# A fused attention and adapter kernel on one core: one group of scores is issued after the next two groups of transposes instead of before them

## The chip, the cores and the metric

The kernel runs on one core of a Trainium2 chip. The metric is the device time of one execution in microseconds; lower is better. Three runs of the kernel before took 963.36, 960.85 and 961.24 us, median 961.24 us.

## What is computed

The reference applies four layers with a residual each to `x` (32 batches of 256 rows by 256 columns). Cut to what matters:

```python
x = x + attention(x, fside, lens)   # 16 heads of 16; q from fside, keys and values from x,
                                    # one own key and value per row, softmax, @ Wo
x = x + layernorm(x + relu(x @ W1[lang] + b1) @ W2[lang] + b2) * gamma[lang] + beta[lang]
x = x + x @ weight[subj].T + bias[subj]
# pooling: scores from a small tanh layer, masked by kind, softmax over 256 keys
a = tanh(x @ W1 + b1) @ v
p = softmax(where(mask[kind], a[None, :], -1e30))
x = x + (p @ x) / mask[kind].sum(-1)
```

## The kernel before, in words

The work is a software pipeline over batches. `steps` calls `step(t, parity)` for t = -2 to 34; t = 6 to 27 run as a loop of two steps a turn, the others are written out. In a steady step six batches are at work at once (`at_work`): A projects queries and keys of batch t+2, B computes row maxima and values for t+1, C the scores, exponentials and the first half of the weighted sums of t, E finishes the attention of t-1, F runs the adapter and the subject's linear layer of t-2, and G the pooling of t-3. From t = 30 on A is off, from t = 31 on B, from t = 32 on C; G is on for t = 3 to 34.

Each engine has its own order, written out by hand in its `step`. Semaphores tie them together. The names that matter here:

- **TensorE (PE).** `scores(pair)`, pair 0 to 7, issues eight matmuls on 64 or 63 rows of the array: four transposed scores of batch t into `ST` (line 515) and four plain scores of batch t+1 into `SN` (line 519), two banks each. It waits for `exp_done` and `maxed`, that is until ScalarE and VectorE have emptied those banks. `weighted(k, ...)` (line 494) is 32 matmuls on column tiles 32 wide that sum the exponentials `pt` with the values `vaug`; `weighted(0)` needs the exponentials of pairs 0 to 3 only. `turn` (line 425) is four 128x128 transposes of a 256x256 tile. The transposes of `pe3`, the pooled probabilities (the third part of the buffer `soft`), go to bank `pT`; those of `att`, the attention rows (buffer `nv`), go to `aT`; those of `yn`, the normalised rows, go to `x2T`. Projections go through `three` (line 417): `values("v", ...)` is 12 matmuls `M<-Wv,xs`, `values("vs", ...)` 12 matmuls `M<-Wv,ss`.
- **ScalarE (ACT).** `unit(s)`, s = 0 to 15, is one exponential `pt<-ST` (line 890); units 2p and 2p+1 belong to pair p. Between them stand copies out of PSUM: `keys_out` (`kf`), the high part of the weights `lwp`, the two exponentials of the pooling (line 1011, each with a second instruction that reads the accumulated sum and whose end raises the semaphore `pe3`), `values_out` (`vaug`), the copy of the transposed probabilities `p3T` (shown as `soft<-M`), of `aT`, and the two `yn` (line 1029).
- **VectorE (DVE).** `unit(s)` is one row maximum `mx<-SN` (line 1132). `fold_join(2)` exists at t = 0 and 1 only.

The order of TensorE around the change, before:

```python
                scores(4)
                ...
                    own_scores()
                    values("v", xs[odd], W["v"])
                scores(5)
                ...
                    pe.wait_ge(sem("pe3"), done(t - 3, 2))
                    turn(bank["pT"], pe3).then_inc(sem("pT_pe"), 1)
                ...
                    turn(bank["aT"], att).then_inc(sem("aT_pe"), 1)
                ...
                    weighted(0, t, par)
                scores(6)
```

Of the kernel before, what the change touches and what calls it, by code (L numbers as in the profile page):

```python
# [74 lines left out]
def done(b, per=1, nth=None):  # L75

    nth = per if nth is None else nth
    if isinstance(b, int):
        return 0 if b < 0 else B * per if b >= B else b * per + nth
    return b * per + nth  # L80
# [7 lines left out]
def before(b, unit):  # L88

    if isinstance(b, int):  # L90
        return max(0, min(b, B) * UNITS + unit) if b < B else B * UNITS
    return b * UNITS + unit


def block4(nc: bass.Bass, x, xsT, lens, ids, wq, wk, wv, wo, wad, lw, lwT, lb, fixed_d, early_d, kidx_d,
           pmask_d, out):
    ctx = ExitStack()
    with ctx:
# [8 lines left out]
        def sem(name):  # L107
            if name not in sems:
                sems[name] = ctx.enter_context(nc.semaphore(name))
            return sems[name]  # L110
# [146 lines left out]
        def folding(t):  # L257

            return isinstance(t, int) and 0 <= t < 2
# [151 lines left out]
        def _(pe):  # L411
# [9 lines left out]
            def turn(dst, src):  # L421

                for c in range(NC2):
                    for i in range(2):
                        last = nc.tensor.transpose(dst[:, c * S + i * P:c * S + i * P + P],  # L425
                                                   src[:, i, c * P:c * P + P], ident[:])
                return last
# [35 lines left out]
            def step(t, par):  # L463
# [3 lines left out]
                def free(name):  # L467

                    k = NAMES.index(name)
                    mine, u = PIECES[k][3], t  # L470
                    while True:
                        k -= 1
                        if k < 0:
                            k, u = len(PIECES) - 1, u - 1
                        if isinstance(u, int) and u < -2:
                            return
                        _, n, o, on_bank = PIECES[k]
                        if on_bank == mine and folding(u) and n in FOLD:
                            pe.wait_ge(cat, 4 * u + FOLD.index(n) + 1)
                            return  # L480
                        if on_bank == mine and (not isinstance(u, int) or 0 <= u + o < B):
                            for s, per, nth in READER[n]:
                                pe.wait_ge(sem(s), done(u + o, per, nth))
                            return
# [14 lines left out]
                def scores(pair):  # L499

                    if on["C"] and pair % PH == 0:
                        pe.wait_ge(sem(f"mput{pair // PH}"), done(t, 64))
                    if on["B"] and pair % PH == 0:
                        pe.wait_ge(sem(f"stack{pair // PH}"), done(t + 1, SK))
                    if on["C"]:
                        pe.wait_ge(sem("exp_done"), before(t, 2 * pair))
                    opening = isinstance(t, int) and t == -1
                    rows_to = ST if opening and pair % 2 else SN
                    if on["B"]:
                        pe.wait_ge(sem("maxed"), max(0, 2 * pair - 2) if opening else before(t + 1, 2 * pair))  # L510
                    for e in range(2):
                        lo_, hi_ = 64 * e, 64 * (1 - e)
                        for half in range(2):
                            if on["C"]:
                                keys = nc.tensor.matmul(ST[e][:, half * S:half * S + S],  # L515
                                                        kst[par][lo_:lo_ + MROW + 1, pair, half * P:half * P + P],
                                                        qst[par][lo_:lo_ + MROW + 1, pair, :], start=True, stop=True)
                            if on["B"]:
                                rows_ = nc.tensor.matmul(rows_to[e][:, half * S:half * S + S],  # L519
                                                         qst[odd][hi_:hi_ + MROW, pair, half * P:half * P + P],  # L520
                                                         kst[odd][hi_:hi_ + MROW, pair, :], start=True, stop=True)
                        if on["C"]:
                            keys.then_inc(sem("st_ready"), 1)
                        if on["B"]:
                            rows_.then_inc(sem("sn_ready"), 1)
# [8 lines left out]
                def values(name, left, w):  # L534

                    for i in range(2):
                        last = three(bank[name][:, i * D:i * D + D], lambda r, c: left[r][:, c, i * P:i * P + P],
                                     lambda r, c: w[r][:, c, :])
                    last.then_inc(sem(f"{name}_pe"), 1)
# [138 lines left out]
                if on["B"]:  # L678
                    own_scores()
                    free("v")  # L680
                    values("v", xs[odd], W["v"])
                scores(5)
                if folding(t):
                    fold_next("pT")
                if on["G"]:
# [3 lines left out]
                if on["E"]:  # L689
                    free("aT")  # L690
                    pe.wait_ge(sem("att"), done(t - 1))
                    turn(bank["aT"], att).then_inc(sem("aT_pe"), 1)
                if on["C"]:
                    weighted(0, t, par)
                scores(6)
# [32 lines left out]


            steps(pe, step)  # L730


# [133 lines left out]
        def _(act):  # L866
            def copy(dst, src, bias=0.0):
                return nc.scalar.activation(dst, src, ACT.Identity, bias=bias)  # L868
# [5 lines left out]
            def halves(name):  # L874
                return bank[name][:].rearrange("p (c q) -> p c q", c=2)

            def step(t, par):
# [3 lines left out]
                def unit(s):  # L881

                    if not on["C"]:
                        return
                    g, j = s // 4, s % 4
                    act.wait_ge(sem("st_ready"), before(t, s + 1))
                    if s % 8 == 0:

                        act.wait_ge(sem("pv_done"), done(t - 1, 2, s // 8 + 1))
                    nc.scalar.activation(pt[:, g, :, j, :],  # L890
                                         ST[s % 2][:].rearrange("p (h q) -> p h q", h=2), ACT.Exp,
                                         scale=SCALE).then_inc(sem("exp_done"), 1)
# [119 lines left out]
                                             accum_out=sum3[:, i:i + 1]).then_inc(sem("pe3"), 1)  # L1012
                if on["B"]:
                    values_out()
                unit(10)
                unit(11)
                if on["G"]:
                    act.wait_ge(sem("pT_pe"), done(t - 3))
                    act.wait_ge(sem("pool_pe"), done(t - 4))
                    copy(p3T[:], halves("pT")).then_inc(sem("p3T"), 1)  # L1020
                if on["E"]:
                    act.wait_ge(sem("aT_pe"), done(t - 1))
                    act.wait_ge(sem("wo_pe"), done(t - 2))
                    copy(aT[0][:], halves("aT")).then_inc(sem("aThi"), 1)
# [27 lines left out]


            steps(act, step)


        @block.vector
        def _(dve):
# [47 lines left out]
            def step(t, par):  # L1106
# [12 lines left out]
                def maxima_turn(half, b, i):  # L1119

                    dve.wait_ge(sem(f"mneg{half}"), done(b))
                    dve.wait_ge(sem(f"mput{half}"), done(b - 1, 64))
                    nc.vector.transpose(mT[half][:], mneg[i][:].bitcast(F32)).then_inc(sem(f"mT{half}"), 1)

                def unit(s):

                    if not on["B"]:
                        return
                    dve.wait_ge(sem("sn_ready"), before(t + 1, s + 1))
                    if s < 2:  # L1130
                        dve.wait_ge(sem("earg"), done(t - 1))
                    nc.vector.tensor_reduce(out=mx[odd][:, :, 8 * (s // 8) + PH * (1 - s % 2) + s // 2 % PH],  # L1132
                                            in_=(ST if isinstance(t, int) and t == -1 and s // 2 % 2 else SN)[s % 2][:].rearrange("p (h k) -> p h k", h=2),
                                            op=ALU.max, axis=AX.X).then_inc(sem("maxed"), 1)
# [29 lines left out]
                def fold_join(j):  # L1164

                    if not folding(t):
                        return
                    name, j = FOLD[j], j + 4 * t
                    dve.wait_ge(fold, j + 1)
                    nc.vector.tensor_tensor(lw3[:, j], bank[name][:, 0:2 * A1].rearrange("p (c n) -> p c n", c=NC2),  # L1170
                                            w3s, ALU.add).then_inc(cat, 1)
# [108 lines left out]
                    nc.vector.bn_aggr(mv[:, 1, :], st[:, 1, :]).then_inc(sem("var"), 1)  # L1280
                if on["B"]:
                    maxima_turn(0, t + 1, odd)
                unit(10)
                unit(11)
                fold_join(2)
                if on["G"]:

                    dve.wait_ge(sem("pe3"), done(t - 3, 2))
# [107 lines left out]
```

## Time and profile before

| what | value |
|---|---|
| median of three runs | 961.24 us (960.85 to 963.36) |
| the profiled execution's own time | 958.85 us |
| its span, first to last instruction | 956.9 us |
| TensorE matmul busy | 915.0 us, 96% |
| VectorE, ScalarE, GpSimd busy | 73%, 67%, 64% |
| granted TensorE clock, mean | 0.979 |

The span is the time between the first and the last instruction of the profiled execution; its own time has 1.95 us more around it, and lies 2.4 us under the median of the runs. Busy time of TensorE is modelled from pipelined matmuls, so 96% says that something is nearly always in the array, and not that it runs at its peak. A timeline row gives the start of a group, how long it lasted, the engine, the line, the operation, the tiles it writes and reads, its shape and how many instructions were merged; an arrow in square brackets tells how long the engine was idle before it and who ended that.

### The profile page before, as it was taken

The numbers are of one execution on the slowest core, as the hardware profiler recorded it, in microseconds if no ns is written. First come the engines' busy times: TensorE is split into PE (matmuls) and PEld (weight loads), VectorE is DVE, ScalarE is ACT, GpSimd is POOL, SyncE is SP. The second block draws the span as 40 slices with busy tenths as digits, with TensorE's granted clock in tenths as the row PEclk, the third lists the DMA queues.
The fourth block names the chain that finished last, engine by engine and source line by source line (L and its number), as shares of the span: only waits on it lengthen the run. The fifth ranks groups of instructions, "written<-read, shape, count | busy, mean of one in ns | idle before, by whom it ended". The sixth has DMA issues, their size and how long they took to land. (4 is left out here: it accounts for less than half of the span.)

```text
span 956.9 us, 27946 instructions
## 1 busy us (share of the span) xinstructions
PE 915.0 (96%) x8564; PEld 764.2 (80%) x8564; DVE 695.3 (73%) x1608; ACT 641.1 (67%) x1377; POOL 608.0 (64%) x771
## 2 busy tenths in 40 slices
PE   8899999999999999999999999999999999999855
PEld 7787788888888888888888888888888888877544
DVE  7765777877777778777777777777777777776442
ACT  2355677777677777776777777767777776677541
POOL 5333777767666777666676766666777676655551
PEclk9999999999999999999999999999999999999876
DMA  5544335344433444444334444443353444432311
GB/s 199 173 138 142 114 110 158 128 147 156 132 126 114 143 142 139 146 145 134 117 122 148 138 133 156 139 130 122 119 156 126 145 156 135 122 108 74 96 43 34
DMA packets 113193, 124.55 MB, mean 130 GB/s; under 512 B 23525, under 2 KB 95094, under 8 KB 113142
## 3 DMA queue, kind: packets, MB, share of 16 engines
q1 hardware_dynamic: 111846, 122.44, 40.5%
q10 hardware_dynamic: 1296, 1.46, 0.5%
q8 instruction: 27, 0.44, 0.2%
q14 instruction: 24, 0.20, 0.1%
HBM read 64.05 MB, written 8.96 MB: 76 GB/s over the span
## 5 line engine op out<-in xcount | busy, mean ns | idle before, releaser
L1132 DVE TENSOR_REDUCE mx<-SN 128x2 f32<-128x512 f32 x504 | 324.1, 685 | 72.4 <-PE SN L519 72.2
L890 ACT ACTIVATE pt<-ST 128x512 f32<-128x512 f32 x512 | 278.1, 599 | 81.1 <-PE ST L515 79.3
L515 PE MATMUL ST<-qst,kst 64*128 64x256 f32 x1024 | 187.9, 305 | 12.2 <-DVE mx L1132 4.5
L515 PEld LDWEIGHTS ST<-qst,kst 64*128 64x128 f32 x1024 | 136.1, 186 | 68.0 <-issue 26.4
L519 PE MATMUL SN<-kst,qst 63*128 63x256 f32 x1008 | 184.2, 305 | 0.1
L519 PEld LDWEIGHTS SN<-kst,qst 63*128 63x128 f32 x1008 | 132.8, 186 | 0.8 <-issue 0.4
L494 PE MATMUL PV<-pt,vaug 128*32 128x256 f32 x2048 | 125.1, 385 | 0.0
L748 POOL TENSOR_TENSOR ss<-xsin,ss 128x512 fp32r<-128x512 f32 x32 | 41.4, 1292 | 121.9 <-ACT ss L868 113.9
L494 PEld LDWEIGHTS PV<-pt,vaug 128*32 128x32 f32 x2048 | 60.4, 110 | 43.7 <-issue 6.6
L417 PE MATMUL M<-lwp,x2T 128*128 128x320 f32 x384 | 70.8, 321 | 1.0 <-DVE ob L1316 1.0
L748 POOL TENSOR_TENSOR x2T<-x2f,x2T 128x512 fp32r<-128x512 f32 x32 | 41.2, 1287 | 44.2 <-ACT x2T L868 44.2
L708 PE MATMUL M<-x,soft 128*128 128x256 f32 x256 | 65.6, 402 | 0.8 <-ACT soft L868 0.8
L748 POOL TENSOR_TENSOR xs<-xsin,xs 128x512 fp32r<-128x512 f32 x31 | 40.0, 1289 | 39.3 <-ACT xs L868 39.3
L791 POOL TENSOR_TENSOR nv<-nv,rec 128x512 f32<-128x512 f32 x32 | 34.0, 1062 | 43.2 <-DVE rec L1152 43.2
L417 PEld LDWEIGHTS M<-lwp,x2T 128*128 128x128 f32 x384 | 58.3, 193 | 1.8 <-DVE ob L1316 1.7
L417 PE MATMUL PV<-Wo,aT 128*128 128x256 f32 x384 | 56.6, 297 | 1.1 <-ACT pvt L868 1.1
L417 PE MATMUL PV<-ss,Wq 128*128 128x256 f32 x384 | 54.1, 291 | 1.9 <-POOL ss L748 1.9
L417 PE MATMUL M<-ss,Wk 128*128 128x256 f32 x384 | 55.3, 295 | 0.0
L868 ACT ACTIVATE qf<-PV,bqc 128x256 f32<-128x256 f32 x64 | 26.9, 471 | 42.4 <-PE PV L417 42.4
L708 PEld LDWEIGHTS M<-x,soft 128*128 128x128 f32 x256 | 49.5, 204 | 7.2 <-issue 1.1
L1161 DVE TENSOR_TENSOR x<-M,lbr 128x320 f32<-128x320 f32 x64 | 31.1, 486 | 32.2 <-PE M L417 32.2
L417 PE MATMUL M<-Wv,ss 128*128 128x256 f32 x384 | 53.8, 289 | 0.0
(140 smaller groups left out, 2088.1 us busy)
## 6 DMA issues: line engine op xcount, KB each, us to landing
qst<-qp SPq DMA_DIRECT2D x186, 128.0 KB
kst<-kp SPq DMA_DIRECT2D x186, 128.0 KB
xsin<-in_xsT SPq DMA_DIRECT2D x31, 512.0 KB, 3.4
adw<-in_wad SPq DMA_DIRECT2D x32, 322.5 KB, 3.9
pm<-in_pmask SPq DMA_DIRECT2D x32, 257.0 KB, 2.7
xr<-in_x SPq DMA_DIRECT2D x32, 256.0 KB, 4.2
lwf<-in_lwT SPq DMA_DIRECT2D x32, 256.0 KB, 3.1
out<-ob SPq DMA_DIRECT2D x32, 256.0 KB, 2.1
```

Of the source, the lines that this page charges most:

```text
L417: last = nc.tensor.matmul(dst, left(a, c), right(b, c), start=n == 0, stop=n == 5)
L494: last = nc.tensor.matmul(PV[32 * j:32 * j + 32, (g % 2) * S:(g % 2) * S + S], vaug[i][:, kb, 4 * g + j, :], pt[:, g, kb, j, :], start=kb ...
L515: keys = nc.tensor.matmul(ST[e][:, half * S:half * S + S], kst[par][lo_:lo_ + MROW + 1, pair, half * P:half * P + P], qst[par][lo_:lo_ + M ...
L519: rows_ = nc.tensor.matmul(rows_to[e][:, half * S:half * S + S], qst[odd][hi_:hi_ + MROW, pair, half * P:half * P + P], kst[odd][hi_:hi_ + ...
L708: last = nc.tensor.matmul(bank["pool"][:, i * D:i * D + D], p3T[:, c, i * P:i * P + P], x3[:, c, 0:D], start=c == 0, stop=c == 1)
L748: return nc.gpsimd.tensor_tensor(dst, src, high.bitcast(F32), ALU.subtract)
L791: nc.gpsimd.tensor_tensor(att[:].rearrange("p c (h d) -> p c h d", d=DH), nv[:].rearrange("p c (h d) -> p c h d", d=DH), rec[:].unsqueeze( ...
L868: return nc.scalar.activation(dst, src, ACT.Identity, bias=bias)
L890: nc.scalar.activation(pt[:, g, :, j, :], ST[s % 2][:].rearrange("p (h q) -> p h q", h=2), ACT.Exp, scale=SCALE).then_inc(sem("exp_done"), 1)
L1132: nc.vector.tensor_reduce(out=mx[odd][:, :, 8 * (s // 8) + PH * (1 - s % 2) + s // 2 % PH], in_=(ST if isinstance(t, int) and t == -1 and ...
L1161: nc.vector.tensor_tensor(x3[:, i, :], bank[f"lin{i}"][:, 0:NX], lbr[:], ALU.add).then_inc(sem("x3"), 1)
```

## The change

On TensorE `scores(5)` is issued behind the transposes of `pe3` and of `att`, directly ahead of `weighted(0)`. On ScalarE the copy `p3T` of the transposed probabilities stands ahead of units 10 and 11, the exponentials of that group of scores. On VectorE `fold_join(2)` stands ahead of its units 10 and 11. No instruction is added or removed, and every wait keeps its value.

```diff
@@ TensorE
                     values("v", xs[odd], W["v"])
-                scores(5)
                 if folding(t):
                     fold_next("pT")
                 if on["G"]:
@@
                     pe.wait_ge(sem("att"), done(t - 1))
                     turn(bank["aT"], att).then_inc(sem("aT_pe"), 1)
+                scores(5)
                 if on["C"]:
                     weighted(0, t, par)
                 scores(6)
@@ ScalarE
                 if on["B"]:
                     values_out()
-                unit(10)
-                unit(11)
                 if on["G"]:
                     act.wait_ge(sem("pT_pe"), done(t - 3))
                     act.wait_ge(sem("pool_pe"), done(t - 4))
                     copy(p3T[:], halves("pT")).then_inc(sem("p3T"), 1)
+                unit(10)
+                unit(11)
                 if on["E"]:
@@ VectorE
                     maxima_turn(0, t + 1, odd)
+                fold_join(2)
                 unit(10)
                 unit(11)
-                fold_join(2)
```

TensorE's queue in a steady step, before, from the values to the weighted sums; a row has the line, the operation, what it writes and reads, its shape and the semaphores it waits for. Of the eight matmuls of the scores the first two are shown:

```order
L417 MATMUL M<-Wv,xs 128x256 [waits y]
L417 MATMUL M<-Wv,xs 128x256 x11
L515 MATMUL ST<-qst,kst 128x256 [waits maxed,exp_done]
L519 MATMUL SN<-kst,qst 128x256
...
L425 MATMUL M<-fixed,soft 128x128 [waits pe3,kf]
L425 MATMUL M<-fixed,soft 128x128 x3
L425 MATMUL M<-fixed,nv 128x128 [waits att,nself]
L425 MATMUL M<-fixed,nv 128x128 x3
L494 MATMUL PV<-pt,vaug 32x256 [waits qf,v,exp_done]
L494 MATMUL PV<-pt,vaug 32x256 x15
```

The same place in the changed kernel:

```order
L417 MATMUL M<-Wv,xs 128x256 [waits y]
L417 MATMUL M<-Wv,xs 128x256 x11
L425 MATMUL M<-fixed,soft 128x128 [waits pe3,kf]
L425 MATMUL M<-fixed,soft 128x128 x3
L425 MATMUL M<-fixed,nv 128x128 [waits att,nself]
L425 MATMUL M<-fixed,nv 128x128 x3
L515 MATMUL ST<-qst,kst 128x256 [waits maxed,exp_done]
L519 MATMUL SN<-kst,qst 128x256
...
L494 MATMUL PV<-pt,vaug 32x256 [waits qf,v,exp_done]
L494 MATMUL PV<-pt,vaug 32x256 x15
```

The eight matmuls of `scores(5)` moved past the eight transposes; the first transpose, which waits for `pe3`, now stands directly behind the values.

ScalarE's queue at the same place of a steady step, before, from the second exponential of pair 4 on:

```order
L890 ACTIVATE pt<-ST 128x2x256 [waits st_ready]
L1011 ACTIVATE soft,sum<-soft,nm 128x256 [waits r3,pT_pe,nm3]
L1011 ACTIVATE soft,sum<-soft,nm 128x256
L868 ACTIVATE vaug<-M 128x32x16 [waits pv_done,v_pe]
L890 ACTIVATE pt<-ST 128x2x256 [waits st_ready] x2
L868 ACTIVATE soft<-M 128x512 [waits pool_pe,pT_pe]
L868 ACTIVATE aT<-M 128x512 [waits wo_pe,aT_pe]
L1029 ACTIVATE yn<-y,shift,rstd 128x256 [waits x2T_pe,shift]
```

And in the changed kernel:

```order
L890 ACTIVATE pt<-ST 128x2x256 [waits st_ready]
L1011 ACTIVATE soft,sum<-soft,nm 128x256 [waits r3,pT_pe,nm3]
L1011 ACTIVATE soft,sum<-soft,nm 128x256
L868 ACTIVATE vaug<-M 128x32x16 [waits pv_done,v_pe]
L868 ACTIVATE soft<-M 128x512 [waits pool_pe,pT_pe]
L890 ACTIVATE pt<-ST 128x2x256 [waits st_ready] x2
L868 ACTIVATE aT<-M 128x512 [waits wo_pe,aT_pe]
L1029 ACTIVATE yn<-y,shift,rstd 128x256 [waits x2T_pe,shift]
```

The copy of the transposed probabilities and the two exponentials of pair 5 have changed places; all that stands ahead of them, the pooling's two exponentials among it, is where it was.

## Rows read from the trace of the kernel before

**Rows 1.** The page: the span, and the busy time of TensorE.

```profile
span 956.9 us, 27946 instructions
PE 915.0 (96%) x8564; PEld 764.2 (80%) x8564; DVE 695.3 (73%) x1608; ACT 641.1 (67%) x1377; POOL 608.0 (64%) x771
```

**Rows 2.** Windows: stretch and its length, busy time by engine, clock, DMA share, GB/s.

```profile
480.00:508.00 28.00, 27.92 (x274) 23.50 (x272) 21.64 (x51) 20.29 (x45) 19.49 (x25) 1.00 0.46 147
860.00:866.00 6.00, 4.85 (x44) 4.07 (x43) 5.96 (x16) 3.99 (x8) 2.57 (x4) 1.00 0.49 161
```

**Rows 3.** Timeline of TensorE in one steady step: start us, us.

```profile
481.67 1.67 PE L417 MATMUL M<-Wv,xs 128*128 128x256 f32 x12
483.27 0.38 PE L515 MATMUL ST<-qst,kst 64*128 64x256 f32 x1
...
483.94 0.66 PE L425 MATMUL M<-fixed,soft 128*128 128x128 f32 x4
...
484.96 1.93 PE L494 MATMUL PV<-pt,vaug 128*32 128x256 f32 x32
486.82 0.38 PE L515 MATMUL ST<-qst,kst 64*128 64x256 f32 x1
...
487.49 0.65 PE L425 MATMUL M<-fixed,yn 128*128 128x128 f32 x4
...
491.89 1.68 PE L417 MATMUL M<-Wv,ss 128*128 128x256 f32 x12
493.41 1.05 PE L417 MATMUL M<-lwp,x2T 128*128 128x320 f32 x6
```

**Rows 4.** Timeline of ScalarE over the same step.

```profile
480.19 0.84 ACT L868 ACTIVATE kf<-M,bkc 128x256 f32<-128x256 f32 x2 [1.12 <-PE M L417]
...
481.54 1.08 ACT L890 ACTIVATE pt<-ST 128x512 f32<-128x512 f32 x2
...
483.39 0.21 ACT L1011 ACTIVATION_READ_ACCUMULATOR soft<-soft,nm 128x1 f32 x1
...
485.39 0.65 ACT L868 ACTIVATE aT<-M 128x512 fp32r<-128x512 f32 x1
485.87 1.14 ACT L1029 ACTIVATE yn<-y,shift,rstd 128x256 f32<-128x256 f32 x2
487.36 1.08 ACT L890 ACTIVATE pt<-ST 128x512 f32<-128x512 f32 x2 [0.34 <-PE ST L515]
488.33 0.60 ACT L868 ACTIVATE pvt<-PV 128x512 f32<-128x512 f32 x1
```

**Rows 5.** Timeline of ScalarE: the sum's last read at t = 3, 30 and 32.

```profile
126.00 0.21 ACT L1011 ACTIVATION_READ_ACCUMULATOR soft<-soft,nm 128x1 f32 x1
866.57 0.19 ACT L1011 ACTIVATION_READ_ACCUMULATOR soft<-soft,nm 128x1 f32 x1
911.75 0.19 ACT L1011 ACTIVATION_READ_ACCUMULATOR soft<-soft,nm 128x1 f32 x1
```

**Rows 6.** Timeline of TensorE: `scores(5)` at t = 3 and 30; t = 31; the transpose at t = 32.

```profile
125.87 0.38 PE L515 MATMUL ST<-qst,kst 64*128 64x256 f32 x1
866.67 0.38 PE L515 MATMUL ST<-qst,kst 64*128 64x256 f32 x1
889.71 0.80 PE L515 MATMUL ST<-qst,kst 64*128 64x256 f32 x4 [1.88 <-ACT pt L890]
890.78 1.09 PE L425 MATMUL M<-fixed,soft 128*128 128x128 f32 x4 [0.27 <-ACT soft L1011]
892.65 0.66 PE L494 MATMUL PV<-pt,vaug 128*32 128x256 f32 x4
912.08 0.77 PE L425 MATMUL M<-fixed,soft 128*128 128x128 f32 x4 [3.75 <-ACT soft L1011]
```

**Rows 7.** Timeline of VectorE in the same step: maxima of pair 5, low part of `aT`.

```profile
483.84 1.29 DVE L1132 TENSOR_REDUCE mx<-SN 128x2 f32<-128x512 f32 x2 [0.24 <-PE SN L519]
...
486.07 0.69 DVE L1137 TENSOR_TENSOR aT<-M,aT 128x512 fp32r<-128x512 f32 x1 [0.67 <-ACT aT L868]
```

## The prediction

> **What bounds the kernel now.** I read the page first, then the busy time by windows, then the timelines of TensorE and ScalarE around the change. The page shows TensorE busy for 915.0 of 956.9 us, and no other engine over 73% [rows 1]. The windows show that the steady part is tighter still: 27.92 of 28 us are busy, at a granted clock of 1.00, the 2.4 GHz level [rows 2]. In the timeline of one steady step the groups follow each other without an idle bracket [rows 3]: values at 481.67, `scores(5)` at 483.27, the transposes of `pe3` at 483.94, the weighted sums at 484.96, `scores(6)` at 486.82, the transposes of `yn` at 487.49. So a steady step costs what TensorE's queue costs. A wait put into that queue costs its whole length, and a wait of another engine costs nothing until TensorE stands behind it. The question is when the things that the moved groups wait for are ready.
>
> **What the first transpose waits for.** It needs `pe3`, the pooling's two exponentials, complete with their sum. ScalarE is woken for this stretch by TensorE itself, at the end of the key projection: `kf` at 480.19 after 1.12 us of idling, then without a pause `lwp`, the two exponentials of pair 4 at 481.54, the pooling's two, and the last read of the sum, which starts at 483.39 and ends at 483.60 [rows 4]. `scores(5)` starts at 483.27, so `pe3` is complete 0.33 us after that start. Today the 0.67 us of `scores(5)` hide it: the transposes start at 483.94, 0.34 us after `pe3`. At t = 3 it is the same: the read ends at 126.21, `scores(5)` starts at 125.87, 0.34 us later than which `pe3` is complete [rows 5, 6]. This distance can't drift, since the chain starts on TensorE's own key projection and has no other wait in it. At t = 30 the chain lacks `kf`, and the read ends at 866.76 against 866.67, 0.09 us [rows 5, 6].
>
> **The change, part by part.** Time zero is the present start of `scores(5)`.
>
> (1) *The lost cover.* The transposes now come where `scores(5)` was, and `pe3` is complete only at 0.33 to 0.34. From that end to the first transpose there is a further delay: at t = 32, where TensorE stands waiting for the same semaphore, the read ends at 911.94 and the transpose starts at 912.08, 0.14 us [rows 5, 6]. I take 0.14; the least would be nothing, the most would be twice that, since no row shows a longer one. The transposes start at 0.33 + 0.14 = 0.47 us.
>
> (2) *The rest of the moved block.* The two groups of transposes took 483.94 to 484.96 = 1.02 us, and `scores(5)` 483.27 to 483.94 = 0.67 us [rows 3]. They only change places: `scores(5)` starts at 0.47 + 1.02 = 1.49, the weighted sums at 1.49 + 0.67 = 2.16. Now they start at 484.96 - 483.27 = 1.69. **TensorE loses 0.47 us a step here.** Of the waits of `scores(5)` itself none is late: the exponentials of pair 4 are through by 482.62 [rows 4], 0.65 us before the place it had already.
>
> (3) *One change of the array's tiling less.* Scores use the array by 64 rows, the weighted sums by 32 columns, the rest as a whole. The order values, scores, transposes, weighted sums changes the form three times, the new one twice. Twelve matmuls take 1.60 us in front of scores (481.67 to 483.27) and 1.52 us in front of other whole-array matmuls (491.89 to 493.41) [rows 3], so a change costs about 0.1 us. Where TensorE doesn't wait, this is a gain. In steps 3 to 29 it isn't one: the change left out is the one ahead of the transposes, and it would fall into the time in which TensorE stands waiting for `pe3` anyway. I count it nought there, and 0.1 us for each of t = 0, 1 and 2, which have no pooling. The Trainium skill, TensorEngine Tiling (Array Packing), section Key Properties, says that a change of tiling mode drains TensorE. By that rule the change is worth 0.1 us a step; the trace agrees with the rule in the pair of 1.60 and 1.52 us, and it is the first rival below.
>
> (4) *What is late next: `yn`.* On ScalarE the copy of `p3T` now comes ahead of the exponentials of pair 5. It is not late: the four transposes are complete 0.66 us after 0.47 [rows 3], a copy like it takes the engine 0.48 us (485.39 to 485.87) [rows 4], so it is through at 1.6, and the exponentials can't start before 1.49 + 0.54 = 2.03. But behind those exponentials stand `aT` and the two `yn`, and they lose time. An exponential starts 487.36 - 486.82 = 0.54 us after its scores; two of them take 488.33 - 487.36 = 0.97 us until the next instruction, `aT` 0.48, both `yn` 1.14 to the end [rows 3, 4]. So `yn` is complete at 1.49 + 0.54 + 0.97 + 0.48 + 1.14 = 4.62, and with the 0.14 us of (1) its transposes can start at 4.76. TensorE is there at 2.16 + 1.86 (weighted sums) + 0.67 (`scores(6)`) = 4.69 [rows 3]. That is a second wait of 0.07 us; between nothing and 0.15 us, since all its terms are rounded. Now `yn` ends at 487.01, 0.48 us ahead of 487.49. The copy of `aT` itself, ready at 3.6, has its reader, the output projection, only after the pooling's matmuls; VectorE's low part of it takes 0.69 us [rows 7] and is in time. The maxima of pair 5 started 0.57 us behind their scores and took 1.29 us [rows 3, 7]; from 1.49 on they end at 3.35, and `scores(6)`, which overwrites their bank, comes at 2.16 + 1.86 = 4.02. What stands behind on ScalarE is again woken by `scores(6)`.
>
> (5) *Other queues.* SP and GpSimd have the same rows. VectorE's moved piece exists at t = 0 and 1 only, and its bank is read earlier than before: nothing.
>
> (6) *The sum.* Steps 3 to 29 (27 of them): 0.47 + 0.07 = 0.54, together 14.6 us. Step 30: `pe3` at 0.09 + 0.14 = 0.23 instead of 0.47, so 0.23 + 0.07 = 0.3 us. Step 31: the four matmuls of `scores(5)` ran from 889.71 while TensorE waited for ScalarE anyway, and took 0.80 us [rows 6]; now they stand behind the same wait, ahead of the weighted sums of 892.65, for 0.4 to 0.8 us: 0.6. Steps 32 to 34 have no scores. Steps 0 to 2: -0.3. Sum: **15.2 us more**. On the profiled execution that is 958.85 + 15.2 = 974.1 us; it was 2.4 us under the median of the runs, and from the median 961.24 it is **976.4 us**, which I give.
>
> **Rivals.**
>
> *The wait does not come about, and the drain is saved.* If `pe3` were in time (because what looks like a chain that ends at 0.33 is released earlier than the end of the read), 31 steps from t = 0 to 30 would gain 0.1 us: 961.2 - 3.1 = 958.1 us, faster. It decides when `pe3` can release TensorE at least 0.33 us before the end of that read. For it: the rule on drains, and the pair 1.60 and 1.52 us [rows 3]. Against it: at t = 32 the transpose came 0.14 us after that end and not ahead of it [rows 5, 6]. 4%.
>
> *The wait is nearly covered.* If only some 0.1 us of it were left, for example because the engine's queue hides more than I see, gain and loss cancel: about 961 us. Only a much shorter chain on ScalarE could do it, and that chain isn't touched. 3%.
>
> *The clock falls.* A wait in every step could bring the clock down. Behind the idle 1.88 us at 889.71 the eight transposes took from 890.78 to 892.65, 1.87 us where they take 1.02 in the steady step; with as much lost again on the weighted sums behind them, some 2 us go with one such event, an estimate from these rows [rows 3, 6]. In 27 steps that is 54 us: about 1030 us. Against it: from 860 to 866 TensorE was busy only 4.85 of 6 us, with the clock still at 1.00 [rows 2]; the new wait leaves it idle for about 0.5 of 28 us. 2%. The Trainium skill, TensorE: Matmul & The Clock Gate, section A second HAM failure mode, describes frequent short idles between groups of matmuls that make the clock swing between its levels; the row of 860 to 866 does not agree with that for idles of this size.
>
> *More is late behind it than I see* (the `yn` wait at 0.15 us or over, or a third wait of that size): 27 times 0.2 us more, 980 to 983 us. 10%.
>
> **How the numbers follow.** The forecast, a wait for `pe3` with a small one for `yn` or none, has the remaining 81%. Without the `yn` wait it gives 961.2 + 13.3 = 974.5; with a release of nothing instead of 0.14 us another 3.8 us less, 970.7; with the release at 0.28 us, 980.2; with `yn` at its upper bound 978.6; and the runs of before spread by 2.5 us. The range of 971 to 981 us holds these and part of the last rival. A measurement of this kernel can tell about 0.3%, some 3 us, from no change. Slower by over 0.3%: 81 + 10 + 2 = 93%. Within: 3%, the second rival. Faster: 4%, the first.
>
> **What would show it.** In the changed profile the first transpose of `pe3` in each steady step starts some 0.14 us after the read of the sum ends, with an idle bracket that names the pooling's exponential, and the values end without one. A step lasts half a us longer. The transposes of `yn` follow ScalarE's `yn` by 0.14 us with a wait of under 0.15 us, or none. ScalarE's idle time ahead of the exponentials of pair 5 grows. The clock stays at 1.00 in steady windows. I am wrong if a step takes no longer than now, if the distance of the weighted sums from the values is as before, or if the loss is at another line.

## The result and the profile after

| | before | changed |
|---|---|---|
| median | 962.04 us (4 runs, 960.85 to 963.36) | 974.68 us (4 runs, 970.52 to 975.52) |
| profiled execution, own time / span | 958.85 / 956.9 us | 975.52 / 973.5 us |
| mean granted clock | 0.979 | 0.975 |

The ratio is 1.0122, 95% interval 1.0099 to 1.0145: slower by 12.6 us between the medians, in the range of 971 to 981 us, 1.7 us under the 976.4 us of the forecast.

The page of the changed kernel answers to [rows 1]:

```profile
span 973.5 us, 27946 instructions
PE 918.3 (94%) x8564; PEld 767.1 (79%) x8564; DVE 714.2 (73%) x1608; ACT 646.6 (66%) x1377; POOL 607.0 (62%) x771
```

TensorE ran the same 8564 matmuls. Its busy time grew by 3.3 us, some of it at half clock (experiment 7), and the span by 16.6 us: for the rest the engine stood still. A window of the steady part, in the columns of [rows 2]:

```profile
480.00:508.00 28.00, 27.51 (x268) 23.05 (x268) 21.88 (x50) 20.10 (x43) 19.03 (x25) 1.00 0.43 134
```

27.51 of 28 us are busy instead of 27.92, at a clock still at 1.00. The place of the loss stands in the timeline of TensorE in one steady step, in the columns of [rows 3]:

```profile
490.52 1.67 PE L417 MATMUL M<-Wv,xs 128*128 128x256 f32 x12
492.60 0.63 PE L425 MATMUL M<-fixed,soft 128*128 128x128 f32 x4 [0.41 <-ACT soft L1011]
493.06 0.60 PE L425 MATMUL M<-fixed,nv 128*128 128x128 f32 x4
493.59 0.38 PE L515 MATMUL ST<-qst,kst 64*128 64x256 f32 x1
...
494.27 1.93 PE L494 MATMUL PV<-pt,vaug 128*32 128x256 f32 x32
496.13 0.38 PE L515 MATMUL ST<-qst,kst 64*128 64x256 f32 x1
...
496.80 0.66 PE L425 MATMUL M<-fixed,yn 128*128 128x128 f32 x4
```

and in that of ScalarE, in those of [rows 4]:

```profile
489.04 0.84 ACT L868 ACTIVATE kf<-M,bkc 128x256 f32<-128x256 f32 x2 [1.12 <-PE M L417]
489.77 0.74 ACT L868 ACTIVATE lwp<-lwf 128x640 fp32r<-128x640 f32 x1
...
492.24 0.21 ACT L1011 ACTIVATION_READ_ACCUMULATOR soft<-soft,nm 128x1 f32 x1
...
493.26 0.60 ACT L868 ACTIVATE soft<-M 128x512 f32<-128x512 f32 x1 [0.32 <-PE M L425]
494.13 1.09 ACT L890 ACTIVATE pt<-ST 128x512 f32<-128x512 f32 x2 [0.27 <-PE ST L515]
495.10 0.61 ACT L868 ACTIVATE aT<-M 128x512 fp32r<-128x512 f32 x1
495.58 1.10 ACT L1029 ACTIVATE yn<-y,shift,rstd 128x256 f32<-128x256 f32 x2
```

The read of the pooling's sum ends at 492.45 and the first transpose starts at 492.60, with an idle bracket that names the pooling's exponential. The values, which had 1.60 us to themselves, now have 2.08. The whole kernel's waits of TensorE (us in total, times, longest) have this wait 4 times before:

```profile
PE M L425 <- ACT soft L1011: 8.8, 4, 3.7
```

and 31 times in the changed kernel, whose three longest sums are:

```profile
PE M L425 <- ACT soft L1011: 22.5, 31, 3.7
PE ST L515 <- DVE mx L1132: 6.5, 14, 1.6
PE M L425 <- ACT yn L1029: 4.8, 3, 1.8
```

**The length of a step.** I take it from the start of `own_scores` at t = 3 and at t = 29, 26 steps apart. Before:

```profile
123.35 0.40 PE L600 MATMUL M<-fixed,pr 128*128 128x16 f32 x2
...
838.03 0.39 PE L600 MATMUL M<-fixed,pr 128*128 128x16 f32 x2
```

Changed:

```profile
126.35 0.40 PE L600 MATMUL M<-fixed,pr 128*128 128x16 f32 x2
...
852.75 0.40 PE L600 MATMUL M<-fixed,pr 128*128 128x16 f32 x2
```

That is 714.68 / 26 = 27.49 us and 726.40 / 26 = 27.94 us: 0.45 us more a step, 12.2 us in the 27 steps from 3 to 29. This number repeats to 0.02 us between executions; the rest of the time doesn't, as experiment 7 shows. All experiments are therefore read twice, by their median and by this step.

### The profile page after: what moved, and what is told of

Same layout as the page of the kernel before. It is cut to its first block and busy times, and to the rows that moved or that the text cites. A ratio compares the mean times of both kernels' runs of the same rounds, so it can differ in the third digit from the quotient of the medians.

```text
span 973.5 us, 27946 instructions
## 1 busy us (share of the span) xinstructions
PE 918.3 (94%) x8564; PEld 767.1 (79%) x8564; DVE 714.2 (73%) x1608; ACT 646.6 (66%) x1377; POOL 607.0 (62%) x771
## 5 line engine op out<-in xcount | busy, mean ns | idle before, releaser
L417 PE MATMUL M<-Wv,xs 128*128 128x256 f32 x384 | 54.1, 291 | 0.1
```

The source lines that it names most:

```text
L417: last = nc.tensor.matmul(dst, left(a, c), right(b, c), start=n == 0, stop=n == 5)
```

## The experiments

The theory: TensorE waits for `pe3`, the end of a chain on ScalarE, in every step; a small second wait for `yn` may follow. Rivals: the new order itself costs (drains, slower transposes behind the values); the clock falls; ScalarE's order, and not TensorE's, makes the difference. Intervals are against the kernel before on the same chip (median 960.93 us of 23 runs for experiments 1 to 4, 960.58 us of 7 runs for 5 and 6). A kernel with lines moved or added has other line numbers: L1006 and L1014 are the pooling's exponentials too, L418 and L426 the projections and the transposes.

**1. The changed kernel with a shorter chain.**

```diff
                 unit(6)
                 unit(7)
                 if on["A"]:
                     keys_out()
-                if on["F"]:
-                    ... copy(lwp[:, 0], lwf[:]).then_inc(sem("lwhi"), 1)
                 unit(8)
                 unit(9)
                 if on["G"]:
                     ...  # the pooling's two exponentials, pe3
+                if on["F"]:
+                    ... copy(lwp[:, 0], lwf[:]).then_inc(sem("lwhi"), 1)
                 if on["B"]:
                     values_out()
```

> The changed kernel, with ScalarE's copy of the high part of the linear weights moved from ahead of the exponentials of pair 4 to behind the pooling's two exponentials. The chain that ends in pe3 becomes 0.62 us shorter. Theory (the loss is TensorE's wait for pe3): the end of the sum's read comes 0.2 us ahead of the place of the transposes, the wait is gone, one change of tiling less is left as a gain; a steady step lasts 27.4 us instead of 27.49 before and 27.93 in the changed kernel, in all 958 to 961 us. Rival (the new order itself costs, by drains or by slower transposes behind the values): 27.9 us a step and 974 us stay.

Measured: 954.03 us, ratio 0.9933 (0.9908 to 0.9957), a step of 27.35 us. TensorE of this kernel:

```profile
478.51 1.68 PE L417 MATMUL M<-Wv,xs 128*128 128x256 f32 x12
480.03 0.60 PE L425 MATMUL M<-fixed,soft 128*128 128x128 f32 x4
480.47 0.60 PE L425 MATMUL M<-fixed,nv 128*128 128x128 f32 x4
481.00 0.38 PE L515 MATMUL ST<-qst,kst 64*128 64x256 f32 x1
...
481.67 1.93 PE L494 MATMUL PV<-pt,vaug 128*32 128x256 f32 x32
```

and its ScalarE:

```profile
479.61 0.21 ACT L1006 ACTIVATION_READ_ACCUMULATOR soft<-soft,nm 128x1 f32 x1
479.70 0.75 ACT L868 ACTIVATE lwp<-lwf 128x640 fp32r<-128x640 f32 x1
```

The read now ends at 479.82, 0.21 us ahead of the transposes, and the idle bracket is gone. The same order of TensorE that cost 12.6 us is now faster than the kernel before. So the order itself costs nothing; the wait did all of it. Without the wait the tiling change that was left out shows: the values take 1.52 us instead of 1.60 and the transposes of `pe3` 0.44 instead of 0.49 [rows 3], 0.14 us together in the mean of the steady steps, and a step is 0.14 us shorter than before. The total came out 4 us under the 958 to 961 us that were expected; the control was 2.9 us faster too, and that is the larger part of it.

**2. The control: the kernel before with the same move of ScalarE's copy.**

> The kernel before with the same move of ScalarE's copy, as the control. Theory: pe3 was hidden behind the sixth group of scores already, so nothing is gained: 27.49 us a step, 961 to 963 us. Rival (ScalarE's order bounds the step in another way, and the copy's place alone is worth something): a step of 27.4 us or less, and the gain of the first experiment would be the copy's and not the moved group's.

Measured: 958.03 us (12 runs), ratio 0.9970 (0.9952 to 0.9987), a step of 27.49 us. The steady step is untouched, as the theory has it: `pe3` was hidden already. The total is 2.9 us lower nevertheless, and that was not expected. In the profiles the difference stands at the end: from `own_scores` of t = 30 to the last instruction it takes 90.3 us, against 93.05 and 93.01 us in two profiles of the kernel before. From t = 32 on no scores are left there, and the chains lie open. At t = 32 the pooling's exponential in this kernel starts when its input is there:

```profile
910.21 0.51 ACT L1006 ACTIVATE soft<-soft,nm 128x256 f32<-128x256 f32 x1 [2.71 <-DVE nm L1256]
```

In the kernel before the exponential's input from VectorE was complete at 909.35, but it stood behind the copy, which started at 910.22 after 3.55 us of idling:

```profile
910.22 0.74 ACT L868 ACTIVATE lwp<-lwf 128x640 fp32r<-128x640 f32 x1 [3.55 <-issue]
910.86 0.49 ACT L1011 ACTIVATE soft<-soft,nm 128x256 f32<-128x256 f32 x1
```

So the transposes of `pe3` of t = 32 start 46.5 us behind `own_scores` of t = 30 instead of 48.2. But this lead of 1.7 us does not last. At t = 33 `yn` waits for GpSimd in the control, and its transposes start at 69.7 us against 69.9:

```profile
933.42 1.09 ACT L1029 ACTIVATE yn<-y,shift,rstd 128x256 f32<-128x256 f32 x2 [1.66 <-POOL shift L823]
```

Nearly all of the 2.7 us comes behind that place, where the same matmuls run at another granted clock. The 12 matmuls of the linear layer of t = 33 ran at 0.50 before (window 939 to 941.5) and at 1.00 in the control:

```profile
939.23 3.57 PE L417 MATMUL M<-lwp,x2T 128*128 128x320 f32 x12 [0.97 <-DVE ob L1316]
```

```profile
939.43 2.02 PE L417 MATMUL M<-lwp,x2T 128*128 128x320 f32 x12 [0.97 <-DVE ob L1316]
```

The same 12 took 3.57 us in two profiles of the unaltered changed kernel and 2.02 us in the third, so one profile can't tell whether the copy's place brings this about. That the copy's move makes the kernel faster is shown by the medians; by which way is open.

Experiment 1 against this control is the price of the moved group alone where its wait is covered: 954.03 against 958.03 us, and 27.35 against 27.49 us a step; 26 to 27 times 0.14 is 3.6 to 3.8 us, of the 4.0 us between the medians.

**3. The changed kernel with a longer chain.**

```diff
+                    act.wait_ge(sem("spared"), done(t - 3))
+                    copy(spare[:], lwf[:]).then_inc(sem("spared"), 1)
                     copy(lwp[:, 0], lwf[:]).then_inc(sem("lwhi"), 1)
```

> The changed kernel with a second copy of the same 640 columns, into a tile that nobody reads, ahead of the real one: the chain to pe3 becomes 0.62 us longer. Theory: every step from 3 to 30 waits 0.62 us more, 28.55 us a step, 975 + 17 = 992 us (989 to 995); the clock stays at 1.00 in the steady part. Rival (the wait is small and the loss lies elsewhere): less than half of that, under 983 us. Rival (clock): the longer idle brings the clock down in the steady part, over 1005 us.

Measured: 991.71 us, ratio 1.0319 (1.0290 to 1.0348), a step of 28.56 us. Its TensorE:

```profile
499.85 1.67 PE L418 MATMUL M<-Wv,xs 128*128 128x256 f32 x12
502.55 0.63 PE L426 MATMUL M<-fixed,soft 128*128 128x128 f32 x4 [1.03 <-ACT soft L1014]
```

The bracket grew from 0.41 to 1.03 us, by the 0.62 us that the copy takes (480.92 to 481.54, [rows 4]), and the step by 28.56 - 27.94 = 0.62 us. And the clock stayed:

```profile
500.00:528.00 28.00, 26.89 (x263) 22.51 (x262) 20.86 (x49) 20.24 (x44) 18.47 (x25) 1.00 0.42 134
```

More than one us of idle time in each step leaves it at 1.00, the 2.4 GHz level. The rival of the clock is out for the steady part. The Trainium skill, TensorE: Matmul & The Clock Gate, section A second HAM failure mode, tells of a kernel in which short idles between groups of matmuls make the clock swing between its levels; with one idle of this size in each step the trace does not show that effect.

**4. The two groups of transposes in the other order.**

```diff
-                if on["G"]:
-                    ... turn(bank["pT"], pe3) ...
                 if on["E"]:
                     ... turn(bank["aT"], att) ...
+                if on["G"]:
+                    ... turn(bank["pT"], pe3) ...
                 scores(5)
```

> The changed kernel with TensorE's two groups of transposes in the other order: attention rows first, pooled probabilities second, then the scores. Theory: the attention rows' 0.46 us cover most of the wait; TensorE waits some 0.1 us instead of 0.57, the weighted sums start 1.67 to 1.75 us after the present place of the scores against 1.69 before; 27.5 to 27.6 us a step, 961 to 965 us. Rival (the order itself costs): as the changed kernel, 974 us.

Measured: 961.31 us, ratio 1.0010 (0.9991 to 1.0029), a step of 27.55 us. Its TensorE:

```profile
481.69 1.68 PE L417 MATMUL M<-Wv,xs 128*128 128x256 f32 x12
483.20 0.60 PE L425 MATMUL M<-fixed,nv 128*128 128x128 f32 x4
483.77 0.63 PE L425 MATMUL M<-fixed,soft 128*128 128x128 f32 x4
...
485.00 1.93 PE L494 MATMUL PV<-pt,vaug 128*32 128x256 f32 x32
```

Covering the wait from TensorE's side does the same as shortening it on ScalarE's: of the 0.57 us between the values' end and the earliest start, some 0.1 us is left (0.57 us for the first group's four transposes instead of 0.44 to 0.49). What is left of the wait and the saved tiling change nearly cancel: 27.55 against 27.49 us a step.

**5. TensorE's part of the change alone.** ScalarE keeps units 10 and 11 ahead of the copy `p3T`, and VectorE keeps `fold_join(2)` behind its units.

> Only TensorE's part of the change; ScalarE keeps the exponentials of pair 5 ahead of the copy of the transposed probabilities. Theory: the same wait for pe3, 0.47 us, and besides the copy now stands between the late exponentials and yn: yn ends 0.48 us later against its transposes, which now wait 0.5 us; 28.4 us a step, 975 + 13 = 988 us. Rival (yn has slack that I didn't see, or the order of the copy doesn't matter): 975 us as the changed kernel.

Measured: 986.86 us, ratio 1.0262 (1.0239 to 1.0285), a step of 28.39 us. Its TensorE:

```profile
497.87 0.63 PE L425 MATMUL M<-fixed,soft 128*128 128x128 f32 x4 [0.40 <-ACT soft L1011]
...
502.48 0.66 PE L425 MATMUL M<-fixed,yn 128*128 128x128 f32 x4 [0.35 <-ACT yn L1029]
```

Both waits show: the one for `pe3` as in the changed kernel, and 0.45 us for `yn` (28.39 - 27.94), which is one copy of 0.48 us more ahead of `yn`, less some 0.03 us. Where TensorE waits for `yn`, its transposes start 0.10 us behind `yn`'s end in the mean of the steady steps (0.05 to 0.145 us), and in the changed kernel 0.135 us: that is the 0.03 us to spare. ScalarE's part of the change is what keeps the second wait away.

**6. ScalarE's and VectorE's parts alone.** TensorE keeps the order of before.

> Only ScalarE's and VectorE's parts of the change; TensorE keeps the order of before. Theory: no wait for pe3, but the copy now waits for the transposes ahead of the exponentials of pair 5, these come 1.15 us later, and yn ends 0.3 to 0.35 us behind the place of its transposes; 27.8 us a step, 962 + 9 = 971 us. Rival (ScalarE's slack swallows it, since it idled before scores 6): 962 us.

Measured: 969.01 us, ratio 1.0082 (1.0059 to 1.0104), a step of 27.75 us. On its ScalarE the copy idles for its transposes and everything behind it is late:

```profile
488.44 0.60 ACT L868 ACTIVATE soft<-M 128x512 f32<-128x512 f32 x1 [0.54 <-PE M L425]
488.93 1.08 ACT L890 ACTIVATE pt<-ST 128x512 f32<-128x512 f32 x2
...
490.36 1.11 ACT L1029 ACTIVATE yn<-y,shift,rstd 128x256 f32<-128x256 f32 x2
```

`yn` ends at 491.47, and its transposes start at 491.52, where they would have followed `scores(6)` at 491.30:

```profile
490.63 0.38 PE L515 MATMUL ST<-qst,kst 64*128 64x256 f32 x1
...
491.52 0.66 PE L425 MATMUL M<-fixed,yn 128*128 128x128 f32 x4 [0.15 <-ACT yn L1029]
```

The 0.22 to 0.27 us are a little less than the 0.3 to 0.35 expected. Each of the two parts alone costs more than nothing, and they belong together; the loss by `pe3` comes from TensorE's part in either case.

**7. Three more profiles, for what varies.** The changed kernel twice and the kernel before once, unaltered.

> The changed kernel again, for what varies between executions. The steady step should be 27.93 to 27.94 us again. Step 2 took 28.96 us in the first profile, with the output projection at half clock, against 27.66 before: if that belongs to the change it comes again; if it is chance, it is 26.3 to 29 us. The same for step 30, where the transposes ran at half clock.

> As the one before: a steady step of 27.93 to 27.94 us; steps 2 and 30 tell whether the stretches at half clock are the change's or chance.

> The kernel before again: 27.49 us a steady step; step 2 26.3 to 29 us if its length is chance, 27.7 us if it is fixed.

| profile | to step 2 | step 2 | a steady step | from step 30 on | span |
|---|---|---|---|---|---|
| before | 95.7 | 27.67 | 27.49 | 93.1 | 956.9 |
| before again | 100.1 | 27.50 | 27.48 | 93.0 | 961.0 |
| changed | 97.4 | 28.95 | 27.94 | 94.5 | 973.5 |
| changed again | 96.5 | 26.29 | 27.94 | 93.5 | 969.1 |
| changed, third | 97.0 | 26.31 | 27.96 | 92.4 | 969.1 |

All in us, from the starts of `own_scores`. The steady step is the same to 0.02 us, and the rest moves with the kernel untouched: by 4.4 us up to step 2, by 2.7 us in step 2, by 2.1 us from step 30 on. In the first profile of the changed kernel the output projection of step 2 ran at half clock:

```profile
106.27 2.93 PE L417 MATMUL PV<-Wo,aT 128*128 128x256 f32 x12 [0.73 <-ACT pvt L868]
```

In the second it took 1.68 us behind a longer idle of 0.84 us:

```profile
104.19 1.68 PE L417 MATMUL PV<-Wo,aT 128*128 128x256 f32 x12 [0.84 <-ACT pvt L868]
```

The first also had an idle of 1.29 us just ahead, at the transposes of `yn`. The control had 1.35 and 0.73 us at the same two places, and its clock did not fall. The transposes of step 30 ran at half clock in the first profile (a window of 882 to 885 has the clock at 0.60) and at full clock in the second. So these stretches are not the change's.

What else sets step 2 stands in the traces: the load of the linear weights `lwf`. It is issued 4.8 us ahead of `own_scores` in all eleven profiles. Where it lands 4.6 to 4.9 us later, GpSimd waits 2.3 us or more for it, `shift` and `yn` come late, and TensorE waits 1.0 to 1.35 us for `yn`; step 2 takes 27.5 us or more (both profiles of before, the control, the changed kernel's first, experiment 3). Where it lands 2.8 to 3.2 us after its issue, TensorE does not wait for `yn`, and step 2 takes 26.3 to 26.5 us (the other six). GpSimd in the kernel before and in the changed kernel's second profile:

```profile
95.74 0.87 POOL L798 TENSOR_TENSOR lwf<-lwf,fixed 128x128 f32<-128x128 f32 x2 [2.46 <-DMA lwf<-lw]
```

```profile
94.99 0.87 POOL L798 TENSOR_TENSOR lwf<-lwf,fixed 128x128 f32<-128x128 f32 x2 [0.86 <-DMA lwf<-lw]
```

The changed kernel has both, so this too is not the change's.

## Why the prediction was right, point by point

- **What bounds the kernel**: right. In each of the six experiments the step came out within 0.1 us of what the reckoning of TensorE's queue gave.
- **(1) The lost cover**: right in mechanism and size. Forecast: the transposes start 0.47 us behind the old start of the scores. Measured: 492.60 - 490.52 = 2.08 us behind the values' start against 1.60, so 0.48. The release of 0.14 us, taken from one row at t = 32, was 0.15 us in the steady step.
- **(2) The rest of the block**: forecast 1.02 + 0.67 = 1.69 us, measured 494.27 - 492.60 = 1.67. The 0.02 us belong to (3): the four transposes of `pe3` take 0.46 instead of 0.49 us, since no tiling change stands ahead of them any more. A wait stands there instead, which is why they don't reach the 0.44 us of experiment 1.
- **(3) The tiling change**: right in kind and priced too low. It was counted nought under the wait and 0.1 us where there is none. Experiment 1 against its control gives 0.14 us for it, and in the changed kernel, from `own_scores` of t = 0 to those of 1 and 2, the two steps take 22.83 and 26.99 us instead of 23.01 and 27.20, some 0.2 us less each (experiment 6, with TensorE's old order, has 23.03 and 27.19). The Trainium skill, TensorEngine Tiling (Array Packing), section Key Properties, says that such a change drains the engine; the 0.14 us agree with it, and the rule taken alone would have forecast a gain.
- **(4) `yn`**: the mechanism is right, and the term was mis-sized. Forecast 0.07 us with 0 to 0.15 as bounds; in the row above the transposes start at 496.80, 0.67 us behind their scores and thus without a wait, and in the mean of the steady steps the wait is 0.01 to 0.02 us, which the transposes behind it make up by being 0.01 us shorter. The two `yn` took 1.10 us instead of the 1.14 of before and began 0.02 us earlier than reckoned. The 0.14 us of release, taken over from the wait for `pe3`, is the longest that is seen for `yn`: experiments 5 and 6 have 0.05 to 0.145 us. Experiments 5 and 6 show how near it stands: 0.48 us more on ScalarE gave 0.45 us a step.
- **(6) The sum**: forecast 14.6 us for steps 3 to 29, measured 12.2. The difference, 2.4 us, is (4) for the most part (27 times 0.07 is 1.9) and (2) for the rest (27 times 0.02). For steps 0 to 2, 30 and 31 I had 0.6 us in sum; the spread there is larger than that. What can be read there agrees roughly: behind `own_scores` of t = 30 the weighted sums start 0.22 us later than before in the second and third profile, forecast 0.23, and those of t = 31 0.96 us later, forecast 0.9. The spans of the profiled pair differ by 16.6 us, 4.4 us more than the steady steps, and the second and third profile of the changed kernel show that this is chance; the medians, 12.6 us apart, agree with the steps. That the total came within 1.7 us of the forecast owes something to luck, since what lies outside the steady steps varies by more than that.
- **The rivals**: the first (no wait, a gain) became true in experiment 1, once the chain was shorter, with 0.14 us a step where I had priced 0.1. The second (nearly covered) is what experiment 4 made, at 961.31 us. The clock did not fall in the steady part, even at more than twice the wait. Of the 10% for more waits behind it nothing came.

## What to carry to other kernels

On an engine that is busy all the time, look up for each moved group when the things it waits for are ready, relative to its new place: here 0.33 us late plus 0.14 us for the release, 27 times. A move that saves a tiling change (0.14 us) can cost more than it saves by uncovering a wait, and then the remedy may lie on the other engine: moving one copy behind the pooling's exponentials turned 12.6 us of loss into a gain of 6.9 us, of which 2.9 us are the copy's own and come without the moved group too. Compare the step's length before comparing totals, since it repeats to 0.02 us where the totals vary by 4 us.

## What the runs showed that I had not expected

- With the copy of the linear weights behind the pooling's exponentials the kernel before is 2.9 us faster, with the steady step unchanged (experiment 2). The profile has the difference at the end, mostly in matmuls that run at full clock there and at half clock before; the cause is open.
- When one load lands decides whether step 2 takes 26.3 or 27.6 us (experiment 7).
- Whether a stretch of the ramp runs at half clock differs from execution to execution: the same 12 matmuls took 2.93 us behind idles of 1.29 and 0.73 us in one, and 1.68 us behind 0.84 us in another, while idles of 1.03 us in every steady step never brought the clock down.
